# Four gated cross-attention layers on one core: later weight preparation, quantisation against a row of scales, and norms of the last feed-forward on ScalarE

## The reference

```python
x = x + tanh(g_xattn[0]) * L0_attention(layernorm(x), ctx)      # 16 heads of 16
x = x + tanh(g_ffn[0])   * L0_bit_ffn(layernorm(x))
x = x + tanh(g_xattn[1]) * L1_attention(layernorm(x), ctx)      # 16 heads of 64
x = x + tanh(g_ffn[1])   * L1_mixture(layernorm(x))             # top 1 of 8 experts
x = x + tanh(g_xattn[2]) * L2_attention(layernorm(x), ctx)
x = x + tanh(g_ffn[2])   * L2_transformer(layernorm(x))         # causal attention + feed-forward
x = x + tanh(g_xattn[3]) * L3_attention(layernorm(x), ctx)
x = x + tanh(g_ffn[3])   * L3_qlora_ffn(layernorm(x))

def act_quant(x):                      # one scale for each token
    scale = 127.0 / clip(max(abs(x), axis=-1, keepdims=True), 1e-05)
    return clip(round(x * scale), -128, 127) / scale
def L0_bit_ffn(x):                     # hidden 1024; weight_quant gives -1, 0, 1 times one scale
    h = act_quant(x) @ weight_quant(w1).T
    h = silu(depthwise_conv1d(h, conv_w, conv_b))
    return act_quant(h) @ weight_quant(w2).T
def L3_qlora_ffn(x):                   # three blocks
    h = x
    for blk in range(3):
        y = gelu(layernorm(qlora(h, 2 * blk)) * gamma[blk] + beta[blk])
        h = h + qlora(y, 2 * blk + 1)
    return h
```

## Time and profile before

| | |
|---|---|
| runs of the kernel | 2917.4 us median of 3 (2917.04 to 2917.83) |
| the profiled execution, its own time | 2892.94 us |
| its span | 2891.7 us |
| PE / DVE / ACT / POOL busy | 92% / 74% / 60% / 39% |
| mean granted clock of TensorE | 0.967 |
| first half, about | 14 to 1330 us |
| second half, about | 1330 to 2610 us |
| last feed-forward with its preparation | 2610 to 2892 us |

### The profile page before, as it was taken

The page is one execution under the profiler, slowest core; times in us unless marked ns, Lnnn a source line. Parts: engine busy times, 40 slices in busy tenths (PEclk is TensorE's granted clock), DMA queues, the critical chain, the costliest instruction groups (busy, mean ns, idle before and its releaser), DMA issues.

```text
span 2891.7 us, 61717 instructions
## 1 busy us (share of the span) xinstructions
PE 2653.2 (92%) x24164; PEld 2160.0 (75%) x24164; DVE 2139.4 (74%) x4730; ACT 1739.2 (60%) x4657; POOL 1139.4 (39%) x1981
## 2 busy tenths in 40 slices
PE   6898989898899989999999999999999999898988
PEld 4677768786777777777777778787788778776776
DVE  6667676777767676777777676777787787866888
ACT  3666767676666666776565455565566565553443
POOL 2232323332444443333544534433333423324665
PEclk8899999999999999999999999999999999998999
DMA  5000000000011121000011211100000001001010
GB/s 183 3 23 10 20 10 16 16 16 16 9 51 47 61 67 47 25 20 19 20 51 47 74 46 48 40 14 18 22 18 16 23 15 33 3 5 33 30 37 23
DMA packets 84091, 92.20 MB, mean 32 GB/s; under 512 B 15252, under 2 KB 77208, under 8 KB 83800
## 3 DMA queue, kind: packets, MB, share of 16 engines
q1 hardware_dynamic: 75352, 59.91, 6.6%
q0 software_dynamic: 8448, 28.34, 3.3%
HBM read 65.36 MB, written 22.85 MB: 31 GB/s over the span
## 4 chain that ended last, share of the span: by engine, by line
PE 64%; DVE 22%; ACT 6%; POOL 4%; issue 3%; DMA 1%; SPq 0%; DVEq 0%; POOLq 0%; ACTq 0%
PE psum L388 15%; PE psum L364 14%; PE psum L357 10%; PE psum L414 7%; PE psum L426 4%; PE psum L381 3%; PE psum L543 3%; PE psum L371 3%; DVE tiny L734 3%; PE psum L378 2%; DVE big L742 2%; DVE big L820 2%; PE psum L537 2%; DVE xn L715 2%; DVE big L824 1%
## 5 line engine op out<-in xcount | busy, mean ns | idle before, releaser
L388 PE MATMUL psum<-ident,big 128*128 128x128 f32 x2816 | 411.1, 283 | 62.3 <-ACT big L1208 32.1
L1208 ACT ACTIVATE big<-big 128x512 f32<-128x512 f32 x512 | 311.3, 632 | 205.3 <-DVE big L742 204.9
L388 PEld LDWEIGHTS psum<-ident,big 128*128 128x128 f32 x2816 | 321.5, 144 | 121.2 <-ACT big L1208 57.7
L734 DVE TENSOR_REDUCE tiny<-psum 128x8 f32<-128x1024 f32 x256 | 312.4, 1220 | 77.7 <-PE psum L414 72.8
L742 DVE TENSOR_TENSOR big<-psum,tiny 128x512 f32<-128x512 f32 x512 | 329.7, 685 | 8.8
L414 PE MATMUL psum<-head_keys,small 64*128 64x256 f32 x2048 | 289.6, 405 | 19.8 <-ACT big L1215 11.7
L1386 POOL TENSOR_SCALAR tiny<-mv 128x1 f32<-128x1 f32 x224 | 54.0, 241 | 635.8 <-DVE mv L705 633.3
L1403 POOL TENSOR_TENSOR head_keys<-big,head_rows 128x512 f32<-128x512 f32 x256 | 263.5, 1049 | 0.0
L1428 POOL TENSOR_TENSOR big<-big,tiny 128x512 f32<-128x512 f32 x128 | 136.8, 1072 | 290.8 <-DVE tiny L777 290.5
L414 PEld LDWEIGHTS psum<-head_keys,small 64*128 64x128 f32 x2048 | 183.9, 189 | 73.6 <-issue 50.7
L1252 ACT ACTIVATE big<-psum,tiny 128x128 f32<-128x128 f32 x512 | 181.7, 383 | 45.2 <-DVE tiny L772 44.6
(11 more groups left out here) (317 smaller groups left out, 6729.7 us busy)
## 6 DMA issues: line engine op xcount, KB each, us to landing
ctxT<-in_ctxT SPq DMA_DIRECT2D x64, 128.0 KB, 2.1
after_L_xattn<-x SPq DMA_DIRECT2D x64, 128.0 KB, 1.7
...
```

Source lines behind the costliest of these rows:

```text
L388: last = pe.transpose(bank[:, k * P:(k + 1) * P], src[:, k * P:(k + 1) * P], identity)
L734: dve.tensor_reduce(top, s8, AX.X, ALU.max).then_inc(*t.dve.tell(p, f"{l}.top{r}"))
L1208: last = act.activation(flat, flat, ACT.Exp, scale=DH ** -0.5)
```

## The change

Three parts, and new `ORDER` strings for all engines (all of them differ from those before).

1. Of the preparation, only `L0`, the quantised weights and `L1` stay at the start. The folding for `L2` and `L3` and the scaling of the weights of `self` become turns of lane 0 ahead of its `bit` stage in passes 1, 3 and 2, with t.b as their bank. Lane 0 of TensorE starts with a wait for `setup.bias_L1`.
2. In `bit`, the second quantisation stays with features on partitions. DVE reduces `t.act_h` over the 8 chunks to 128 x 128 (`pm`), TensorE transposes this one tile, DVE reduces it over its free dimension, and `ident` times the reciprocals (`diag2`) is multiplied by ones to spread the scales along the free dimension of a bank. DVE multiplies `t.act_h` with that bank and rounds by adding and taking off the large number, to bf16.
3. In `L3f`, POOL also makes -mean times rstd, and ACT applies each norm as scale and bias.

```diff
 FREE = {...}
+LATE_AT = {(1, "bit"): "L2", (2, "bit"): "self", (3, "bit"): "L3"}
...
 def pe_bitlinear(pe, m, t, p, l):
+    yield from pe_late(pe, m, t, p, l)
...
-    for half, bank in enumerate((t.a, t.b)):
-        pe.wait_ge(*t.dve.at(p, f"{l}.silu{half}"))
-        transposes(pe, bank, t.act_h[:, 4 * half:4 * half + 4, :].rearrange("p k s -> p (k s)"), 4, m.ident[:]
-                   ).then_inc(*t.pe.tell(p, f"{l}.aT{half}"))
-        yield
-    for half, bank in enumerate((t.a, t.b)):
-        pe.wait_ge(*t.dve.at(p, f"{l}.xi{half}"))
-        transposes(pe, bank[:, 0:2 * P].bitcast(BF16), t.xi[:, half * BANK:(half + 1) * BANK], 4, m.ident_bf[:]
-                   ).then_inc(*t.pe.tell(p, f"{l}.xT{half}"))
-        yield
-    pe.wait_ge(*t.act.at(p, f"{l}.xT1"))
+    pe.wait_ge(*t.dve.at(p, f"{l}.pm"))
+    transposes(pe, t.a, t.peak, 1, m.ident[:]).then_inc(*t.pe.tell(p, f"{l}.pT"))
+    yield
+    pe.wait_ge(*t.dve.at(p, f"{l}.diag2"))
+    pe.matmul(t.b[:, 0:S], m.ones[:], t.diag2, start=True, stop=True).then_inc(*t.pe.tell(p, f"{l}.rows2"))
+    yield
+    pe.wait_ge(*t.dve.at(p, f"{l}.xi1"))
     tokens(pe, t.a, t.xiT, m.w["w2q"], D, chunks=HID0 // P).then_inc(*t.pe.tell(p, f"{l}.out"))
...
 def pe_lane(pe, m, t):
     if t.n == 0:
-        pe.wait_ge(*m.s.dve.at(0, "setup.bias_L3"))
+        pe.wait_ge(*m.s.dve.at(0, "setup.bias_L1"))
...
 def dve_bitlinear(dve, m, t, p, l):
...
+    yield from dve_late(dve, m, t, p, l)
...
-    for half, bank in enumerate((t.a, t.b)):
-        dve.wait_ge(*t.pe.at(p, f"{l}.aT{half}"))
-        dve.tensor_reduce(t.tiny[:, 5 + half:6 + half], bank, AX.X, ALU.max, apply_absolute_value=True
...
-    dve.wait_ge(*t.dve.at(p, f"{l}.am1"))
-    then(dve.tensor_tensor(mx, t.tiny[:, 5:6], t.tiny[:, 6:7], ALU.max), "mx2")
+    dve.wait_ge(*t.dve.at(p, f"{l}.silu1"))
+    dve.tensor_reduce(t.peak, t.act_h.rearrange("p k s -> p s k"), AX.X, ALU.max, apply_absolute_value=True
+                      ).then_inc(*t.dve.tell(p, f"{l}.pm"))
+    yield
+    dve.wait_ge(*t.pe.at(p, f"{l}.pT"))
+    then(dve.tensor_reduce(mx, t.a[:, 0:S], AX.X, ALU.max), "am")
     then(dve.tensor_scalar(mx, mx, 2e-5, 1.0 / 127.0, ALU.max, ALU.mult), "mx2c")
-    dve.reciprocal(rs, mx).then_inc(*t.dve.tell(p, f"{l}.rcp2"))
+    then(dve.reciprocal(rs, mx), "rcp2")
+    dve.tensor_scalar(t.diag2, m.ident[:], rs, None, ALU.mult).then_inc(*t.dve.tell(p, f"{l}.diag2"))
     dve.tensor_scalar(sc, mx, m.deq[:, 1:2], None, ALU.mult).then_inc(*t.dve.tell(p, f"{l}.sc2"))
     yield
+    dve.wait_ge(*t.pe.at(p, f"{l}.rows2"))
     for half in range(2):
-        cols = slice(half * BANK, (half + 1) * BANK)
-        dve.wait_ge(*t.act.at(p, f"{l}.rnd{half}"))
-        dve.tensor_scalar(t.xi[:, cols], t.rounded[:, cols], -MAGIC, None, ALU.add
+        sl = slice(4 * half, 4 * half + 4)
+        dve.tensor_tensor(t.act_h[:, sl, :], t.act_h[:, sl, :],
+                          t.b[:, 0:S].rearrange("p (o s) -> p o s", o=1).to_broadcast([P, 4, S]), ALU.mult
+                          ).then_inc(*t.dve.tell(p, f"{l}.z{half}"))
+    for half in range(2):
+        sl = slice(4 * half, 4 * half + 4)
+        dve.wait_ge(*t.dve.at(p, f"{l}.z{half}"))
+        dve.tensor_scalar(t.xiT[:, sl, :], t.act_h[:, sl, :], MAGIC, -MAGIC, ALU.add, ALU.add
                           ).then_inc(*t.dve.tell(p, f"{l}.xi{half}"))
...
+def dve_late(dve, m, t, p, l):
+
+    if t.n or (p, l) not in LATE_AT:
+        return
+    of, w = LATE_AT[(p, l)], m.w
...
+    dve_fold(dve, m, of).then_inc(*m.late.dve.tell(0, f"late.fold_{of}"))
+    yield
+    dve.wait_ge(*m.late.pe.at(0, f"late.o_{of}"))
+    dve.tensor_copy(m.out_bias[of][:], t.b[:, 0:D]).then_inc(*m.late.dve.tell(0, f"late.bias_{of}"))
+    yield
...
 def act_bitlinear(act, m, t, p, l):
...
-    for half, bank in enumerate((t.a, t.b)):
-        if half == 0:
-            act.wait_ge(*t.dve.at(p, f"{l}.rcp2"))
-        act.activation(t.rounded[:, half * BANK:(half + 1) * BANK], bank, ACT.Identity, bias=m.magic[:, 0:1],
-                       scale=t.tiny[:, 3:4]).then_inc(*t.act.tell(p, f"{l}.rnd{half}"))
-        yield
...
+def act_norm(act, m, t, p, l, src, dst, name, sub=""):
+
+    act.wait_ge(*t.pool.at(p, f"{l}.nm{sub}"))
+    act.activation(dst, src, ACT.Identity, bias=t.tiny[:, 2:3], scale=t.tiny[:, 1:2]).then_inc(*t.act.tell(p, f"{l}.{name}"))
+    yield
...
 def act_lane_b(act, m, t):
     l = "L3f"
     for p in range(PASSES_B):
+        yield from act_norm(act, m, t, p, l, t.x_in[:], t.h[:], "h")
...
+            yield from act_norm(act, m, t, p, l, t.y[:], t.xn[:], f"xn{b}", b)
...
+def pool_factor(pool, m, t, p, l, sub=""):
+
+    shift = t.tiny[:, 2:3]
+    yield from pool_rstd(pool, m, t, p, l, sub)
+    pool.tensor_scalar(shift, t.mv[:, 0:1], -1.0, None, ALU.mult).then_inc(*t.pool.tell(p, f"{l}.sh{sub}"))
+    pool.wait_ge(*t.pool.at(p, f"{l}.sh{sub}"))
+    pool.tensor_tensor(shift, shift, t.tiny[:, 1:2], ALU.mult).then_inc(*t.pool.tell(p, f"{l}.nm{sub}"))
+    yield
```

More of the change, by code:

```diff
@@ L228 @@
+        "00100311133333000000"
     ),
     "act": (
[L230 to L233 removed]
@@ L624, in pe_lane @@
         if p == 0:
-            pe.wait_ge(*m.s.dve.at(0, "setup.norms"))
+            pe.wait_ge(*m.late.dve.at(0, "late.down"))
         yield from pe_cross(pe, m, t, p, "L2")
@@ L628, in pe_lane, with pe_late @@
         if p == 0:
-            pe.wait_ge(*m.s.dve.at(0, "setup.bias_L3"))
+            pe.wait_ge(*m.late.dve.at(0, "late.bias_L3"))
         yield from pe_cross(pe, m, t, p, "L3")
+def pe_late(pe, m, t, p, l):
+    if t.n or LATE_AT.get((p, l)) not in ("L2", "L3"):
+        return
+    of = LATE_AT[(p, l)]
+    pe.wait_ge(m.loads[of], m.loaded[of])
+    pe.wait_ge(*t.dve.at(p + FREE[l][0], FREE[l][1]))
+    pe.wait_ge(*m.late.dve.at(0, f"late.fold_{of}"))
+    pe_fold(pe, m, of, t.b).then_inc(*m.late.pe.tell(0, f"late.o_{of}"))
+    yield
 def pe_fold(pe, m, l, bank):
-    pe.wait_ge(*m.s.dve.at(0, f"setup.fold_{l}"))
     if l != "L1":
@@ L638, in pe_fold @@
             pe.matmul(bank[:, 0:D], m.bvb[:, k, :], m.w[l + "o"][:, k, :], start=k == 0, stop=False)
-    pe.matmul(bank[:, 0:D], m.ones[0:1, :], m.w[l + "bo"][:], start=l == "L1", stop=True
-              ).then_inc(*m.s.pe.tell(0, f"setup.o_{l}"))
+    return pe.matmul(bank[:, 0:D], m.ones[0:1, :], m.w[l + "bo"][:], start=l == "L1", stop=True)
 def pe_constants(pe, m):
@@ L706, in dve_norm @@
     yield
+def dve_norm(dve, m, t, p, l, src, dst):
+    yield from dve_moments(dve, m, t, p, l, src)
     if tile_of(t.n, p, l):
@@ L1020, in dve_fold @@
             last = dve.tensor_copy(m.bvb[:, k, :], w[l + "bv"][:, k:k + 1].to_broadcast([P, P]))
-    last.then_inc(*m.s.dve.tell(0, f"setup.fold_{l}"))
+    return last
 def dve_bias(dve, m, l):
@@ L1026, in dve_bias @@
     dve.tensor_copy(m.out_bias[l][:], m.setup_bank[:, 0:D]).then_inc(*m.s.dve.tell(0, f"setup.bias_{l}"))
+def dve_late(dve, m, t, p, l):
+    if t.n or (p, l) not in LATE_AT:
+        return
+    of, w = LATE_AT[(p, l)], m.w
+    if of == "self":
+        for name, n in (("selfq", 0), ("selfk", 0), ("selfv", 0), ("gate", 1), ("up", 1)):
+            for k in range(KD):
+                last = dve.tensor_scalar(w[name][:, k, :], w[name][:, k, :], m.norms[:, n, k:k + 1], None, ALU.mult)
+        last.then_inc(*m.late.dve.tell(0, "late.norms"))
+        yield
+        dve.tensor_scalar(w["down"][:], w["down"][:], m.gf["L2"], 0.5, ALU.mult, ALU.mult
+                          ).then_inc(*m.late.dve.tell(0, "late.down"))
+        yield
+        return
+    dve_fold(dve, m, of).then_inc(*m.late.dve.tell(0, f"late.fold_{of}"))
+    yield
+    dve.wait_ge(*m.late.pe.at(0, f"late.o_{of}"))
+    dve.tensor_copy(m.out_bias[of][:], t.b[:, 0:D]).then_inc(*m.late.dve.tell(0, f"late.bias_{of}"))
+    yield
 def dve_constants(dve, m):
@@ L1067, in dve_constants @@
     last.then_inc(*m.s.dve.tell(0, "setup.plan"))
-    yield
-    dve_fold(dve, m, "L2")
-    yield
-    dve_bias(dve, m, "L2")
-    dve.tensor_scalar(w["down"][:], w["down"][:], m.gf["L2"], 0.5, ALU.mult, ALU.mult
-                      ).then_inc(*m.s.dve.tell(0, "setup.down"))
-    yield
-    for name, n in (("selfq", 0), ("selfk", 0), ("selfv", 0), ("gate", 1), ("up", 1)):
-        for k in range(KD):
-            last = dve.tensor_scalar(w[name][:, k, :], w[name][:, k, :], m.norms[:, n, k:k + 1], None, ALU.mult)
-    last.then_inc(*m.s.dve.tell(0, "setup.norms"))
-    yield
-    dve_fold(dve, m, "L3")
-    yield
-    dve_bias(dve, m, "L3")
     yield
@@ L1748, in shared_memory @@
         keep_signals(m.s, e, Signals(sem(e + "_setup"), names))
+    m.late = Lane()
+    for e in ("pe", "dve"):
+        keep_signals(m.late, e, Signals(sem(e + "_late"), [(0, f"late.{n}") for n in LATE[e].split()]))
     groups = ("L0", "L0 ffn", "L1", "router", "L2", "L3")
```

282 lines of the change are left out of this document (137 added, 145 removed), and 6 rows, old and new, of the table STAGE.

## The result

The changed kernel takes 2972.47 us (median of 4 runs, 2967.53 to 2976.90) against 2917.61 before (4 runs): a ratio of 1.0186, 95% interval 1.0168 to 1.0205, **some 55 us slower**. The prediction was 2888, faster.

The account below looks back on a forecast made before the run. PE was taken to bound the first and second half, POOL to replace DVE as fullest in the last feed-forward. Terms -8 - 25 + 4 = -29 gave 2863.9 us profiled, 2888 for the median; range 2862 to 2914, 8 in 10.

Parts of the forecast that it names:

- PE's 92% is nearer to the first: -25: First half: part 2 gains 32 us if PE bounds throughout, 14 by chain shares; 25 us faster taken.
- Rival 2: First half: DVE takes back PE's saving, only 14 us gained; POOL costs 11; 2914 us in all; chance 0.10.
- 1.214 us: `bit` stage: time of DVE's 1024-to-128 reduction, taken from a PSUM reduction of as many elements to 8; 39 us in all.
- rival 3: `bit` stage: the stepped reduction takes twice 1.214 us; 2897 us, or 2927 were DVE the bound; chance 0.12.
- the chain share of 22%: DVE's part of the chain that ended last in the profile before, used to weigh added DVE time.
- PE's saving was set at 32 us: `bit` stage: cheaper transposes save PE 1.0 us a sample over 32 samples.
- +4 was taken: Last feed-forward: part 3 costs 4 us, the middle of 4 us shorter and 11 longer.
- rival 4: Last feed-forward: POOL's queue holds up all lanes and PE waits, stretch +48 us; 2932 us in all; chance 0.08.
- the +11 as the upper end: Last feed-forward: 267 us of POOL if it has gaps as PE has in the second half, 11 longer.
- The -8: Start: later preparation lets lane 0 work while PE waits, 8 us faster.
- I cost these at 0: Passes 1 to 3: lane 0's two added waits for its moved folds cost nothing.
- the signs given: Profile values expected after the change; forecast wrong if first-half PE idle grows over 20 us or POOL idles over 30.

Follow-up runs that it names:

- e_level: `e_parts12` with its first reduction reading elements in the order they lie and without the products with the spread scales; 1.0051 of before.
- e_peback: `e_parts12` with nine float32 128x128 transposes a sample put in ahead of that of the maxima; 1.0179 of before.
- e_parts12: The changed kernel with before's last feed-forward, code and orders, so only parts 1 and 2 and their orders; 1.0116 of before.
- e_flat: `e_parts12` with the first reduction reading its 1024 elements in the order they lie; 1.0053 of before.
- e_part3: The kernel before with part 3 alone and the change's orders for the last feed-forward; 1.0052 of before.
- e_onestep: `e_part3` with -mean times rstd made in one POOL instruction instead of two; 0.9966 of before.

## Why the prediction was wrong

**Part 2, the bound (the step that failed first).** The text read "PE's 92% is nearer to the first: -25", that is, PE is the bound of the first half and what it saves comes off the time. This takes for granted that PE's idle time stays as it is. Instead it grew by 52 us in after (131 to 183), at waits for all three other engines, and the first half became 38 us longer with parts 1 and 2 on the same chip. With DVE near its old level and PE relieved (`e_level`) PE's idle time is still 30 us longer than in before's first half. It was not that PE's work counts for nothing: put back in `e_peback`, it cost 18. A busy share of 92% said that PE is seldom idle, not that its idle time won't grow. Under `e_parts12`'s orders 60 us more on DVE cost 61 and 9 transposes a sample 18; in before, a step that takes 0.2 us more on ScalarE than it did on DVE, 64 times, cost 19. What was taken away came back in part: 22 us of the reduction gave 18, half of GpSimd's normalisation 16 in before, 41 us of the products 1. Rival 2 saw this in kind, DVE taking back what PE gives, and priced it too low.

**Part 2, the sizes.** The reduction was costed at 1.214 us and took 1.907, +22 us: rival 3, which had the right mechanism. 18 us of the loss, give or take 10, hang on it, where the chain share of 22% would give 5; the shares of the chain were no exchange rate between engines. It is 1.58 times a contiguous reduction of as many elements (1.206 in the same place). The note on cachelines that the prediction named (the Trainium skill, "SBUF — State Buffer", "Door 1: The DMA port swizzle", a penalty for accesses that fall in different 16-byte lines) is borne out in its direction by these two figures. The 128x128 reduction (0.280 predicted and measured), the diagonal (0.390 against 0.333) and the products (0.678) were right. PE's saving was set at 32 us. At the same granted clock of 0.95 the first half has 1213.80 us of PE in before and 1189.22 in `e_flat`, 25 less, so the size was about right; at the 0.94 of after only 6 of it show.

**Part 3.** +4 was taken, +13.6 measured in `e_part3` (264.7 to 278.3), and the mis-sized term is the factor on POOL: 1.43 us start to start, 1.58 in fact. Most of the difference is one gap. In before the next instruction starts 0.54 us after the power has started (2628.87 - 2628.33), in after the sign step starts 0.65 after it (2699.45 - 2698.80). The new steps take 0.33 and 0.30 from start to start, not 0.31 and 0.28. Why the gap is there in one case and not in the other was not shown. With 1.58 the need is 271 us instead of 252, and the stretch to be expected was 15 longer. POOL packed without waiting, so the mechanism was the forecast's own (POOL replaces DVE), not rival 4's starved queue, and the +11 as the upper end was too low. That lanes' waits go to ScalarE by way of POOL showed as predicted.

**Part 1.** The -8 was called the middle of -16 and +4, which is -6. Lane 0's first matmul on `w_L0k` came at 52.87 us instead of 114.00, and the first `bit` stage of all ended 7 us earlier, as predicted. But PE is busy 16.04 of 30 us from 60 to 90, not above 20, and the lead of 32 us that the fourth sample has in after is down to 5 at the tenth and gone at the fifteenth. So the step that failed is to count a gain at the start as a gain at the end. "I cost these at 0" for the moved folds is in doubt too: in before's own orders they cost 14 us, while under the changed orders leaving them out gains nothing.

**The second half** was right: 0 give or take 5, measured +5.7 on one chip and +0.2 on another (1255.5 in `e_onestep`, 1255.7 in `e_flat`). **Against the signs given**: PE's idle time in the first half grew by 52 us (the limit was 20), DVE's share is 74% instead of 77% because the stretch is longer, the reduction, 1.907, lies nearer to "above 2" than to 1.2, POOL has 226 us, DVE 176, ACT 175.

In sum, from the runs: part 3 +15, the stepped reduction +18 (give or take 10), and about +15 of the first half that neither DVE's level nor the late work explains, and whose cause stays open; together 48, with 55 measured.
